# A gather that adds into the node's own rows, and another order of conv 2, in a three-layer graph network kernel

## The chip, the cores and the metric

The kernel runs on one NeuronCore of one Trainium2 chip. The time is device time in microseconds (us) of one launch; smaller is better. Of several runs the median is given.

## What is computed

The graph has 30,000 nodes of 512 float32 features and 30,000 edges, sorted by destination. Three graph convolutions follow each other, each of which multiplies with a 512 x 512 matrix and sums over a node and its incoming edges:

```python
h = jnp.maximum(_layernorm(x, axis=-1), 0.0)
x = x + _L0_gnn_ref(h, ...)      # conv 1 and conv 2, below
h = jnp.maximum(_layernorm(x, axis=-1), 0.0)
x = x + _L1_gnn_ref(h, ...)      # conv 3

# _L0_gnn_ref
h = gcn_conv(x, W1, b1, src, dst, N)
h = layer_norm(h, gamma1, beta1)
h = jax.nn.gelu(h, approximate=False)
h = gcn_conv(h, W2, b2, src, dst, N)
h = layer_norm(h, gamma2, beta2)
return jax.nn.gelu(h + residual, approximate=False)

# gcn_conv
msg = (dinv[s] * dinv[d])[:, None] * (x @ W)[s]
out = jax.ops.segment_sum(msg, d, num_segments=n_nodes) + b
```

`s` and `d` hold the edges and one self-loop for each node.

## The kernel before, in words

Setup (some 440 us) counts degrees, builds lists of the rows to gather, splits the weights into a high and a low float32r part (`Whi`, `Wlo`) and writes the first layer's scaled input `H[0]` to HBM.

Then each convolution goes over 118 pairs of tiles; a pair is 2 x 128 nodes, and p is its number. One step on one pair is called a turn here. The rows are summed before they are multiplied with W:

- SyncE (SP) loads the pair's own rows (`self`, 512 KB), `load_self`; in conv 2 and 3 also rows of x.
- GpSimd (POOL) issues three gathers of 128 rows of 2 KB each, `gather`: for the nodes j = 0 and j = 1 of each partition the row of the node's first edge, and a third one with the rows of all further edges, which reach `v`. It also makes two sums in conv 2 and conv 3 (`residual`) and one small power (`power`) in conv 1 and 2.
- ScalarE (ACT) splits the further edges' rows (`vhi`, `over_high`), splits the aggregate out of PSUM (`ahi`, `high`), and does gelu and relu.
- VectorE (DVE) makes `vlo` and the selection matrix `sv` (`over_low`), the aggregate's low part `alo` (`low`), in conv 1 and conv 3 the add of first edges to own rows (`add_first`), the statistics of a product (`stats`, `mean_var`, `var_eps`), and writes (out - mean) * gamma (`centre`), then `normal`. In conv 2 it makes a second layernorm's sums as well (`x2_sum` to `x2_coefs`). In conv 3 only `result` follows the product.
- TensorE (PE) in `aggregate` transposes the own rows (8 products of 128 columns; 16 in conv 2, where the first edges are transposed and accumulated too) and adds the V products (8 of 256 columns, `sv` with `vhi` and `vlo`). In `multiply` it makes 24 products of 512 columns and, in conv 1 and 2, two more with `root` for the bias.

Each engine has a `body(p, known)` written by hand; what it calls in which order is the engine's program, and one turn calls for pair p + 2 what other functions do for p. TensorE's is:

```python
if has(known, 1):
    aggregate(p.after(1))
if has(known, 0):
    for j in range(2):
        multiply(p, j, known)
```

`stats(p)` waits for `multiply(p)`; the V products of `aggregate(p)` wait for `over_low(p)`; `low(p)` gives `multiply(p)` its last third. Aggregates have two buffers in PSUM, products 2 x 2. At each convolution's start all engines wait for each other.

Of the kernel before, what the change touches and what calls it, by code (L numbers as in the profile page):

```python
# [5 lines left out]
P = 128  # L6
ALU = mybir.AluOpType
# [6 lines left out]
EPS = 1e-5  # L14
# [41 lines left out]
def gnn_kernel(nc, x, src, dst, W1, b1, g1, be1, W2, b2, g2, be2, W3, b3, out):  # L56
# [19 lines left out]
    with ExitStack() as ctx:  # L76
# [48 lines left out]
        ones = sb("ones", [P, P])  # L125
# [8 lines left out]
        neg_half = sb("neg_half", [P, 4])  # L134
        dinv = sb("dinv", [P, NTE])
# [6 lines left out]
        has_first = sb("has_first", [P, NTE])  # L142
# [7 lines left out]
        SelfP = [sb(f"self{u}", [P, 2, D]) for u in range(2)]  # L150
        G = [sb(f"g{u}", [P, 3, D]) for u in range(2)]
# [23 lines left out]
        scr = [g[:, :, :].rearrange("p k d -> p (k d)")[:, k * WINDOW:(k + 1) * WINDOW] for g in G for k in range(4)]  # L175
        edge_place = scr[4][:, 0:3 * NPAIR].rearrange("p (c n) -> p c n", c=3)
        fl = G[1][:, 0, :].rearrange("p (h j) -> p h j", h=2)
        b_hi, b_lo = Vhi[0][0:3, :], G[1][0:3, 1, :]
# [5 lines left out]
        oh_place = [sb(f"oh_place{u}", [P, WINDOW], BF16) for u in range(4)]  # L184
# [10 lines left out]
        stage = [t[:, j, :] for t in SelfP for j in range(2)]  # L195
# [16 lines left out]
        g_clear, zero_out = sem("gathered_cleared"), sem("zeros_out")  # L212
# [28 lines left out]
        with nc.Block() as block:  # L241
            @block.sync
            def _(sp):
# [61 lines left out]
            def _(pool):  # L305
# [22 lines left out]
                pool.wait_ge(win_turned, 1)  # L328
                nc.gpsimd.memset(G[0][:, :, :], 0.0).then_inc(g_clear, 1)
                pool.wait_ge(place_used, 3 * NPAIR)  # L330
                nc.gpsimd.memset(G[1][:, :, :], 0.0)
# [25 lines left out]
            def _(dve):  # L357
# [9 lines left out]
                nc.vector.memset(has_first[:, :], 0.0)  # L367
# [170 lines left out]
                def place(n):  # L538
                    p, c = n // 3, n % 3
                    if n >= 4:  # L540
                        dve.wait_ge(place_used, n - 3)
                    nc.vector.tensor_scalar(oh_place[n % 4][:, :], placeb[:, :], edge_place[:, c, p:p + 1], None,
                                            ALU.is_equal).then_inc(place_made, 1)
# [12 lines left out]
                link(nc.vector.tensor_scalar(row[:, 3:4], row[:, 0:1], float(N), None, ALU.add))  # L556
                for k in range(3):
# [4 lines left out]
                    if k < 2:  # L562
                        nc.vector.tensor_copy(has_first[:, :].rearrange("p (n j) -> p j n", j=2)[:, k, :], tab[:, 3, :])
# [691 lines left out]
```

## Time and profile before

| | us |
|---|---|
| median of 3 runs (3600.72 to 3601.57) | 3601.41 |
| the profiled execution | 3601.81 |
| its span, first to last instruction | 3599.8 |
| TensorE busy | 3057.2 (85%) |
| VectorE busy | 3139.7 (87%) |
| ScalarE busy | 1650.5 (46%) |
| GpSimd busy | 2095.7 (58%) |
| conv 1, about | 440 to 1403 |
| conv 2, about | 1403 to 2558 |
| conv 3, about | 2558 to 3600 |

In the profile's rows PE is TensorE's products, PEld its weight loads, DVE VectorE, ACT ScalarE, POOL GpSimd, SP SyncE. A row of the timeline has the start, the duration, the engine, the line of the kernel, the operation, and what it writes <- reads; `x4` is four instructions of a kind, merged. In brackets stands how long the engine stood idle before, and who released it. Shares are means over stages with different limits, so the stages are read one by one.

### The profile page before, as it was taken

To read this page: it belongs to the slowest core of one execution; us is meant where nothing else is said; L and a number is where in the kernel's file an instruction comes from. 1 tells how busy PE (TensorE), PEld (TensorE's weight loads), DVE (VectorE), ACT (ScalarE), POOL (GpSimd) and SP (SyncE) were. 2 spreads that over 40 slices of the span, in tenths; PEclk is the share of its full clock that TensorE was granted. 3 is DMA by queue.
4 is the path that set the end of the run, shared out by engine and by line. 5 is a ranking of instruction groups with operands and counts; after the bars stand their busy time and mean duration, and the time that the engine had idled before them with its cause. 6 is when DMAs were issued, how large, how long until landed. Compare 5 with 4: busy or idle time off the path is not lost. (4 is left out here: it accounts for less than half of the span.)

```text
span 3599.8 us, 61879 instructions
## 1 busy us (share of the span) xinstructions
PE 3057.2 (85%) x16897; PEld 2498.2 (69%) x16897; DVE 3139.7 (87%) x6745; ACT 1650.5 (46%) x2375; POOL 2095.7 (58%) x1853
## 2 busy tenths in 40 slices
PE   8133299999999997999999999999488888888888
PEld 2022188888888886777777777778477777777777
DVE  9899789999999996888888888888688888888887
ACT  0366445555555553777777777777311111111111
POOL 0122256556556654677777777777466666666665
PEclk9999999999999998999999999999799999999999
DMA  3499967777777775888888888888477777777775
GB/s 118 163 408 418 365 215 221 220 225 222 218 223 223 220 219 171 289 295 299 297 296 295 296 298 295 297 295 288 162 241 246 241 246 242 241 246 238 246 240 190
DMA packets 277302, 914.70 MB, mean 254 GB/s; under 512 B 47617, under 2 KB 49511, under 8 KB 277246
## 3 DMA queue, kind: packets, MB, share of 16 engines
q1 hardware_dynamic: 191614, 683.15, 53.1%
q0 software_dynamic: 85632, 230.90, 22.9%
q8 instruction: 24, 0.39, 0.0%
q14 instruction: 32, 0.26, 0.0%
HBM read 653.47 MB, written 308.59 MB: 267 GB/s over the span
## 5 line engine op out<-in xcount | busy, mean ns | idle before, releaser
L840 POOL DMA_INDIRECT g<-H,idx x1062 | 1212.3, 1142 | 614.8 <-issue 428.9
L895 ACT ACTIVATE ahi<-agg 128x1024 fp32r<-128x1024 f32 x354 | 360.9, 1019 | 1039.1 <-PE agg L1171 1039.1
L1189 PE MATMUL out<-Whi,ahi 128*128 128x512 f32 x2832 | 768.9, 393 | 0.0
L1189 PE MATMUL out<-Wlo,ahi 128*128 128x512 f32 x2832 | 763.6, 391 | 0.0
L1189 PE MATMUL out<-Whi,alo 128*128 128x512 f32 x2832 | 761.2, 391 | 0.5 <-DVE alo L1006 0.5
L1162 PE MATMUL agg<-ident,self 128*128 128x128 f32 x2832 | 474.5, 279 | 220.9 <-DVE self L998 171.9
L1189 PEld LDWEIGHTS out<-Wlo,ahi 128*128 128x128 f32 x2832 | 531.6, 188 | 119.6
L1189 PEld LDWEIGHTS out<-Whi,alo 128*128 128x128 f32 x2832 | 531.6, 188 | 114.1 <-DVE alo L1006 1.0
L1189 PEld LDWEIGHTS out<-Whi,ahi 128*128 128x128 f32 x2832 | 510.4, 189 | 91.1
L1162 PEld LDWEIGHTS agg<-ident,self 128*128 128x128 f32 x2832 | 339.3, 142 | 315.8 <-DVE self L998 220.6
L1171 PE MATMUL agg<-sv,vhi 128*128 128x256 f32 x1416 | 384.0, 304 | 66.2 <-DVE sv L986 66.2
L902 ACT ACTIVATE y<-y 128x1024 f32<-128x1024 f32 x236 | 250.1, 1060 | 403.2 <-DVE y L1052 403.2
L1006 DVE TENSOR_TENSOR alo<-agg,ahi 128x1024 fp32r<-128x1024 f32 x354 | 427.8, 1208 | 7.5 <-ACT ahi L895 7.5
L865 POOL TENSOR_TENSOR small<-small,neg_half 128x2 f32<-128x2 f32 (+1 forms) x237 | 207.9, 877 | 372.5 <-DVE small L1030 366.2
L986 DVE TENSOR_SCALAR sv<-col,over_to 128x256 fp32r<-128x256 f32 x354 | 420.9, 1189 | 0.0
L984 DVE TENSOR_TENSOR vlo<-g,vhi 128x512 fp32r<-128x512 f32 x354 | 248.8, 703 | 183.6 <-ACT vhi L889 183.6
L851 POOL TENSOR_TENSOR r<-r,vec 128x512 f32<-128x512 f32 x236 | 299.7, 1288 | 141.2 <-ACT r L925 141.2
L1171 PE MATMUL agg<-sv,vlo 128*128 128x256 f32 x1416 | 355.3, 283 | 0.0
L1171 PEld LDWEIGHTS agg<-sv,vhi 128*128 128x128 f32 x1416 | 270.5, 191 | 90.0 <-DVE vlo L984 90.0
L1037 DVE SCALAR_TENSOR_TENSOR conv<-out,small,vec 128x512 f32<-128x512 f32 x472 | 331.1, 743 | 0.0
L858 POOL TENSOR_TENSOR r<-x,vec 128x512 f32<-128x512 f32 x236 | 299.1, 1293 | 10.2 <-DVE conv L1097 7.5
L1014 DVE BATCH_NORM_STATS2 small<-out 128x6 f32<-128x512 f32 x472 | 302.6, 679 | 2.0 <-PE out L1194 2.0
(175 smaller groups left out, 4137.5 us busy)
## 6 DMA issues: line engine op xcount, KB each, us to landing
self<-H SPq DMA_DIRECT2D x351, 512.0 KB, 5.1
H<-ho SPq DMA_DIRECT2D x250, 512.0 KB, 4.2
x<-in_x_dram SPq DMA_DIRECT2D x165, 512.0 KB, 6.2
X<-x SPq DMA_DIRECT2D x117, 512.0 KB, 4.3
x<-X SPq DMA_DIRECT2D x117, 512.0 KB, 7.2
out_dram<-conv SPq DMA_DIRECT2D x117, 512.0 KB, 6.3
H<-x SPq DMA_DIRECT2D x48, 512.0 KB, 9.6
g<-H,idx POOLq DMA_INDIRECT x1062, 4.3
```

The costliest lines, as they stand in the source:

```text
L840: pool.indirect_dma_start(g[:, c, :], None, H[q][0:end, :], bass.IndirectOffsetOnAxis(ap=own[:, c:c + 1], axis=0), bounds_check=end - 1, o ...
L851: nc.gpsimd.tensor_tensor(R[:, j, :], R[:, j, :], beta_b[1][:, :], ALU.add)\
L858: nc.gpsimd.tensor_tensor(R[:, j, :], Xt[:, j, :], bias_b[2][:, :], ALU.add)\
L895: nc.scalar.activation(Ahi[p.slot(2)][:, :], Agg[p.slot(2)][:, :], ACT.Copy)\
L902: nc.scalar.activation(y, y, ACT.Gelu).then_inc(gelu_done.sem, 1)
L986: nc.vector.tensor_scalar(Sv[p.slot(2)][:, :], col[:, :], over_to[:, bass.ds(p.n, 1)], None, ALU.is_equal).then_inc(sv_made.sem, 1)
L1006: nc.vector.tensor_tensor(Alo[p.slot(2)][:, :], Agg[p.slot(2)][:, :], Ahi[p.slot(2)][:, :].bitcast(F32), ALU.subtract).then_inc(lo_done.se ...
L1014: s = nc.vector.bn_stats(m[:, 6 * j:6 * j + 6], Out[2 * p.slot(2) + j][:, :])
L1037: nc.vector.scalar_tensor_tensor(CvP[p.slot(2)][:, j, :], Out[2 * p.slot(2) + j][:, :], m[:, 12 + 2 * j:13 + 2 * j], gamma_b[q][:, :], ALU ...
L1162: nc.tensor.matmul(o, own[:, j, fs], ident[:, :], is_transpose=True, start=(f % 2 == 0 and j == 0), stop=False, skip_group_check=True)
L1171: m = nc.tensor.matmul(agg[:, 2 * f * P:2 * (f + 1) * P], V[p.slot(2)][:, f * P:(f + 1) * P], Sv[p.slot(2)][:, :], start=False, stop=(V is ...
L1189: m = nc.tensor.matmul(o, a[u][:, c:c + P], w[q][:, f, :], start=(n == 0), stop=(third and n == 3 * KD - 1))
```

## The change

The gather of first edges becomes an accumulating one: each gathered row is added by the DMA to the node's own row in SBUF, after the own rows have landed (`compute_op` add). Nodes without a first edge get an index out of bounds, which the DMA skips; before, it fetched a row of zeros for them in conv 1 and 2. So `add_first`, the second eight transposes of conv 2 and the writing of zero rows in setup are gone. The own rows get four buffers, not two, and are loaded a turn earlier; the gather waits for `self_in` and `vlo_done`, no longer for the aggregate or the sum. Several `tensor_scalar` of VectorE become `scalar_tensor_tensor` with a tensor of ones, `sv` among them. In conv 1 `low` moves behind `stats`. In conv 2 the bodies of VectorE, ScalarE and GpSimd are written in another order. Setup uses three buffers in place of four for `oh_place`.

```diff
-        SelfP = [sb(f"self{u}", [P, 2, D]) for u in range(2)]
-        G = [sb(f"g{u}", [P, 3, D]) for u in range(2)]
+        gathered = sb("gathered", [P, 10, D])
+        SelfP = [gathered[:, 2 * u:2 * u + 2, :] for u in range(4)]
+        V = [gathered[:, 8 + u, :] for u in range(2)]
...
-                sp.wait_ge(g_clear, 1)
-                for q in range(3):
-                    sp.dma_start(H[q][N:N + P, :], G[0][:, 0, :]).then_inc(zero_out, 16)
-                sp.wait_ge(zero_out, 16 * 3)
...
                     def load_self(known, p, k):
-                        if has(known, k - 2):
-                            sp.wait_ge(agg_done.sem, agg_done.upto(p.after(-2)))
+                        if has(known, k - 4):
...
-                        sp.dma_start(filled(SelfP[p.slot(2)], last), whole(H[q], p.n, last, general_reg * ROWS))\
+                        sp.dma_start(filled(SelfP[p.slot(4)], last), whole(H[q], p.n, last, general_reg * ROWS))\
...
+                        if has(known, 4):
+                            load_self(known, p.after(4), 4)
...
                         if has(known, k - 2):
-                            if added:
-                                pool.wait_ge(sum_done.sem, sum_done.upto(p.after(-2)))
-                                pool.wait_ge(vlo_done.sem, vlo_done.upto(p.after(-2)))
-                            else:
-                                pool.wait_ge(agg_done.sem, agg_done.upto(p.after(-2)))
+                            pool.wait_ge(vlo_done.sem, vlo_done.upto(p.after(-2)))
                         pool.wait_ge(idx_made.sem, idx_made.upto(p))
+                        pool.wait_ge(self_in.of(p), self_in.upto(p))
                         pool.sem_inc(gather_go, 1)
-                        own, g = idx[p.slot(4)], G[p.slot(2)]
-                        for c in range(3):
-                            end = N + P if padded_rows and c < 2 else N
-                            pool.indirect_dma_start(g[:, c, :], None, H[q][0:end, :],
+                        own = idx[p.slot(4)]
+                        rows = [SelfP[p.slot(4)][:, 0, :], SelfP[p.slot(4)][:, 1, :], V[p.slot(2)][:, :]]
+                        for c, op in enumerate((ALU.add, ALU.add, ALU.bypass)):
+                            pool.indirect_dma_start(rows[c], None, H[q][0:N, :],
                                                     bass.IndirectOffsetOnAxis(ap=own[:, c:c + 1], axis=0),
-                                                    bounds_check=end - 1, oob_is_err=False)\
+                                                    bounds_check=N - 1, oob_is_err=False, compute_op=op)\
                                 .then_inc((g_in if c < 2 else v_in).of(p), 16)
 
...
+                            residual(known, p)
+                        if second and (has(known, 0) or has(known, -2)):
+                            power(p)
                         if has(known, 3):
                             gather(known, p.after(3), 3)
-                        if second and has(known, 0):
-                            residual(known, p)
                         if third and has(known, 1):
                             residual(None if known is None else known + 1, p.after(1))
-                        if (first and has(known, 0)) or (second and (has(known, 0) or has(known, -1))):
+                        if first and has(known, 0):
                             power(p)
...
-
-                    def add_first(p):
-
-                        own, g = SelfP[p.slot(2)], G[p.slot(2)]
-                        dve.wait_ge(self_in.of(p), self_in.upto(p))
...
-                                                                   own[:, j, :], ALU.mult, ALU.add)
-                        s.then_inc(sum_done.sem, 1)
+                        nc.vector.scalar_tensor_tensor(Sv[p.slot(2)][:, :], col[:, :], over_to[:, bass.ds(p.n, 1)],
...
                             for k in range(2):
                                 over_low(p.after(k))
-                                if added:
-                                    add_first(p.after(k))
-                            low(p)
-                        if second and has(known, -2):
-                            x2_coefs(p.after(-2))
-                        if not third and has(known, -1):
+                                if k == 0:
+                                    low(p)
+                        if second:
+                            if has(known, 1):
+                                low(p.after(1))
+                            if has(known, 0):
+                                stats(p)
+                                mean_var(p)
+                            if has(known, -2):
+                                v = x2_var_eps(p.after(-2))
+                                if not has(known, 0):
+                                    v.then_inc(ve_done.sem, 1)
+                            if has(known, 0):
+                                var_eps(p)
+                                centre(p)
+                            if has(known, 2):
+                                over_low(p.after(2))
+                            if has(known, -2):
+                                x2_coefs(p.after(-2))
+                            if has(known, 0):
+                                normal(known, p)
+                            if has(known, 4):
+                                indices(p.after(4))
+                            if has(known, -1):
+                                x2_sum(of(known, -1), p.after(-1))
+                                x2_mean(p.after(-1))
...
+                        if first and has(known, -1):
                             normal(of(known, -1), p.after(-1))
                         if has(known, 4):
                             indices(p.after(4))
-                        if has(known, 2):
-                            over_low(p.after(2))
-                            if added:
-                                add_first(p.after(2))
...
                         if has(known, 0):
                             stats(p)
-                        if second and has(known, -1):
...
+                            low(p.after(1))
                         if has(known, 0):
                             mean_var(p)
-                        if second and has(known, -1):
-                            v = x2_var_eps(p.after(-1))
-                            if not has(known, 0):
-                                v.then_inc(ve_done.sem, 1)
```

VectorE, conv 2, before: one turn in the steady part, from the statistics on (`x,small` ahead of it, not shown, is `x2_sum`; `y` is `normal`, `conv` is `centre`):

```order
L1014 BN_STATS small<-out 128x6 x2
L1072 TENSOR_SCALAR small<-small 128x2
L1023 BN_AGGR small<-small 128x2 x2
L1079 TENSOR_SCALAR small<-small 128x2
L1030 TENSOR_TENSOR small<-small,eps 128x2
L1037 SCALAR_TENSOR_TENSOR conv<-out,small,vec 128x512 x2
L1085 TENSOR_TENSOR small<-small,dinv 128x2
L1088 TENSOR_TENSOR small<-small 128x2
L1052 SCALAR_TENSOR_TENSOR y<-conv,small,r 128x512 x2
L978 COPY idx<-rows_from 128x3
L984 TENSOR_TENSOR vlo<-g,vhi 128x512
L986 TENSOR_SCALAR sv<-col,over_to 128x256
```

The same engine and convolution in the changed kernel:

```order
L993 TENSOR_TENSOR alo<-agg,ahi 128x1024
L1001 BN_STATS small<-out 128x6 x2
L1010 BN_AGGR small<-small 128x2 x2
L1066 SCALAR_TENSOR_TENSOR small<-small,eps_c 128x2
L1017 TENSOR_TENSOR small<-small,eps 128x2
L1024 SCALAR_TENSOR_TENSOR conv<-out,small,vec 128x512 x2
L985 TENSOR_TENSOR vlo<-gathered,vhi 128x512
L987 SCALAR_TENSOR_TENSOR sv<-col,over_to,ones 128x256
L1072 TENSOR_TENSOR small<-small,dinv 128x2
L1075 TENSOR_TENSOR small<-small 128x2
L1039 SCALAR_TENSOR_TENSOR y<-conv,small,r 128x512 x2
L979 COPY idx<-rows_from 128x3
```

`alo` of pair p + 1 now opens the turn. `vlo` and `sv` are for pair p + 2 in both, but before they were made in the body ahead of the statistics of p, and now in the same body behind the statistics and `conv` of p.

TensorE, conv 2, in the changed kernel: from the transposes of pair p + 2 to the first product of p + 1, with the semaphores waited for. The order is that of before but for the eight transposes of `g`, which are gone:

```order
L1157 MATMUL agg<-ident,gathered 128x128 [waits g_in3]
L1157 MATMUL agg<-ident,gathered 128x128 x7
L1164 MATMUL agg<-sv,vhi 128x256 [waits sv_made,vlo_done]
L1164 MATMUL agg<-sv,vlo 128x256
L1164 MATMUL agg<-sv,vhi 128x256
L1164 MATMUL agg<-sv,vlo 128x256
L1164 MATMUL agg<-sv,vhi 128x256
L1164 MATMUL agg<-sv,vlo 128x256
L1164 MATMUL agg<-sv,vhi 128x256
L1164 MATMUL agg<-sv,vlo 128x256
L1182 MATMUL out<-Whi,ahi 128x512 [waits cg_done,hi_done]
```

Nothing moved here: TensorE still makes the aggregate of p + 2 between the products of p and those of p + 1.

VectorE, conv 3, before: one turn.

```order
L978 COPY idx<-rows_from 128x3
L984 TENSOR_TENSOR vlo<-g,vhi 128x512
L986 TENSOR_SCALAR sv<-col,over_to 128x256
L998 SCALAR_TENSOR_TENSOR self<-g,has_first,self 128x512 x2
L1006 TENSOR_TENSOR alo<-agg,ahi 128x1024
L1097 SCALAR_TENSOR_TENSOR conv<-out,dinv,r 128x512 x2
```

And in the changed kernel:

```order
L985 TENSOR_TENSOR vlo<-gathered,vhi 128x512
L987 SCALAR_TENSOR_TENSOR sv<-col,over_to,ones 128x256
L979 COPY idx<-rows_from 128x3
L993 TENSOR_TENSOR alo<-agg,ahi 128x1024
L1084 SCALAR_TENSOR_TENSOR conv<-out,dinv,r 128x512 x2
```

The two adds into `self` are gone, `idx` stands behind `sv`, and `sv` reads one tensor more.

## Rows read from the trace of the kernel before

**Rows 1.** Windows of conv 1, 2, 3: busy us (instructions), clock, DMA share, GB/s.

```profile
core 0: us, PE busy (x) PEld busy (x) DVE busy (x) ACT busy (x) POOL busy (x), PEclk, DMA share, GB/s
600.00:900.00 300.00, 299.54 (x1575) 247.59 (x1574) 285.55 (x529) 152.54 (x189) 179.24 (x152) 1.00 0.74 223
1500.00:1800.00 300.00, 281.35 (x1581) 238.59 (x1579) 256.50 (x663) 215.24 (x347) 215.66 (x191) 1.00 0.87 297
2700.00:3000.00 300.00, 260.19 (x1390) 215.12 (x1388) 258.73 (x279) 53.98 (x70) 191.24 (x173) 1.00 0.75 243
```

**Rows 2.** Timeline of conv 1, TensorE: transposes of two turns early and two late.

```profile
502.39 1.03 PE L1162 MATMUL agg<-ident,self 128*128 128x128 f32 x8
...
510.21 1.03 PE L1162 MATMUL agg<-ident,self 128*128 128x128 f32 x8
...
1300.02 1.09 PE L1162 MATMUL agg<-ident,self 128*128 128x128 f32 x8
...
1307.97 1.09 PE L1162 MATMUL agg<-ident,self 128*128 128x128 f32 x8
```

**Rows 3.** Timeline of one turn of conv 2, TensorE and VectorE.

```profile
1903.15 0.68 DVE L984 TENSOR_TENSOR vlo<-g,vhi 128x512 fp32r<-128x512 f32 x1
...
1903.75 0.38 DVE L986 TENSOR_SCALAR sv<-col,over_to 128x256 fp32r<-128x256 f32 x1
...
1904.27 0.36 PE L1171 MATMUL agg<-sv,vhi 128*128 128x256 f32 x1 [0.57 <-DVE sv L986]
...
1906.39 1.28 DVE L1014 BATCH_NORM_STATS2 small<-out 128x6 f32<-128x512 f32 x2
...
1911.05 0.40 PE L1194 MATMUL out<-B,root 128*128 128x512 f32 x1
...
1911.29 0.27 PE L1162 MATMUL agg<-ident,self 128*128 128x128 f32 x1
...
1913.77 0.35 PE L1171 MATMUL agg<-sv,vhi 128*128 128x256 f32 x1 [0.57 <-DVE sv L986]
```

**Rows 4.** Timeline of conv 1's end: TensorE's last product, VectorE behind it.

```profile
1392.98 0.39 PE L1194 MATMUL out<-B,root 128*128 128x512 f32 x1
...
1393.41 0.70 DVE L1014 BATCH_NORM_STATS2 small<-out 128x6 f32<-128x512 f32 x1 [1.28 <-PE out L1194]
...
1394.61 1.40 DVE L1037 SCALAR_TENSOR_TENSOR conv<-out,small,vec 128x512 f32<-128x512 f32 x2
```

**Rows 5.** Timeline of one turn of conv 3.

```profile
2957.59 2.96 DVE L986 TENSOR_SCALAR sv<-col,over_to 128x256 fp32r<-128x256 f32 x1
2957.84 2.55 POOL L858 TENSOR_TENSOR r<-x,vec 128x512 f32<-128x512 f32 x2
...
2961.93 1.09 PE L1162 MATMUL agg<-ident,self 128*128 128x128 f32 x8 [1.09 <-DVE self L998]
```

**Rows 6.** Windows of one microsecond around changes of the granted clock.

```profile
1395.00:1396.00 1.00, 0.00 (x0) 0.00 (x0) 1.00 (x2) 0.00 (x0) 0.47 (x1) 0.71 1.00 414
1419.00:1420.00 1.00, 1.00 (x10) 1.00 (x9) 0.00 (x0) 0.89 (x1) 0.03 (x1) 0.84 0.00 0
2586.00:2587.00 1.00, 0.00 (x0) 0.00 (x0) 1.00 (x1) 0.00 (x0) 1.00 (x2) 0.84 0.65 248
2593.00:2594.00 1.00, 1.00 (x5) 0.80 (x5) 0.00 (x0) 0.82 (x1) 0.97 (x2) 0.75 0.49 131
```

**Rows 7.** Timeline: TensorE's first products after two long idle stretches.

```profile
1413.72 0.45 PE L1162 MATMUL agg<-ident,self 128*128 128x128 f32 x1 [20.35 <-DMA g<-H,idx]
...
2589.47 1.97 PE L1162 MATMUL agg<-ident,self 128*128 128x128 f32 x8 [5.29 <-DVE self L998]
```

**Rows 8.** Groups of GpSimd, conv 3, 2900 to 3100: busy, mean ns | idle before.

```profile
L840 POOL DMA_INDIRECT g<-H,idx x69 | 69.2, 1002 | 70.9 <-issue 41.7 <-DVE self L998 29.2
```

**Rows 9.** DMA queues of the same stretch: packets, MB, share of 16 engines.

```profile
q1 hardware_dynamic: 10063, 36.66, 54.5%
q0 software_dynamic: 5517, 12.15, 20.6%
```

**Rows 10.** DMA issues of the page: size, us from issue to landing.

```profile
self<-H SPq DMA_DIRECT2D x351, 512.0 KB, 5.1
```

More of the change, by code:

```diff
@@ L734, in convolution @@
             first, second, third = q == 0, q == 1, q == 2
-            added = not second
-            padded_rows = not third
             lag = 2 if second else 1
@@ L810, in body @@
                             load_x(known, p.after(2), 2)
-                        if has(known, 3):
-                            load_self(known, p.after(3), 3)
                         if has(known, -lag):
@@ L847, in residual @@
                         R, Xt = RP[p.slot(2)], XtP[p.slot(4)]
+                        if second and has(known, -2):
+                            pool.wait_ge(mean2_done.sem, mean2_done.upto(p.after(-2)))
                         for j in range(2):
@@ L928, in squares @@
                     def squares(p):
-                        m = small[p.after(1).slot(4)]
+                        m = small[p.after(2).slot(4)]
                         for j in range(2):
@@ L938, in relu_x2 @@
                     def relu_x2(known, p):
-                        m = small[p.after(1).slot(4)]
+                        m = small[p.after(2).slot(4)]
                         wait_stored(known, p)
@@ L1056, in x2_sum @@
                     def x2_sum(known, p):
-                        m = small[p.after(1).slot(4)]
+                        m = small[p.after(2).slot(4)]
                         dve.wait_ge(gelu_done.sem, gelu_done.upto(p))
@@ L1132, in body @@
                             stats(p)
-                        if second and has(known, -1):
-                            x2_mean(p.after(-1))
+                        if has(known, 1):
+                            low(p.after(1))
                         if has(known, 0):
                             mean_var(p)
-                        if second and has(known, -1):
-                            v = x2_var_eps(p.after(-1))
-                            if not has(known, 0):
-                                v.then_inc(ve_done.sem, 1)
-                        if has(known, 0):
                             var_eps(p)
@@ L1210, in convolution @@
                 landed.close()
-            if added:
-                sum_done.close()
             if not third:
@@ L1216, in convolution @@
                 for flag in (ve_done, rstd_done):
-                    flag.close(NPAIR + second)
+                    flag.close(NPAIR + 2 * second)
                 root_in.close()
```

146 lines of the change are left out of this document (70 added, 76 removed).

## The prediction

> **What bounds the kernel now.** I read the windows first. In conv 1 TensorE is busy 299.5 of 300 us, in conv 2 281.4, in conv 3 260.2, while VectorE has 285.6, 256.5 and 258.7 [rows 1]. A "turn" below is the work on one pair of tiles; each convolution has 118. TensorE issues 42, 50 and 40 products a turn, so the counts of the windows give turns of 8.00, 9.49 and 8.63 us.
>
> Then the timeline, for what each turn waits on. Conv 1 is TensorE itself: where nothing holds it a turn is 510.21 - 502.39 = 7.82 us, later 1307.97 - 1300.02 = 7.95 because the own rows wait a little for VectorE's add [rows 2]. In conv 2 a turn is 1913.77 - 1904.27 = 9.50 us. The wait that ends last is TensorE's for `sv` (0.57 us at line 1171) [rows 3]. The reader should note one thing more there: VectorE starts its statistics at 1906.39, and they read the product whose last instruction (`root`) stood a turn before 1911.05, at 1901.55. VectorE comes more than four microseconds behind TensorE, so TensorE does not wait for statistics. In conv 3, `sv` takes 2.96 us while GpSimd makes its two sums (2.55 us), the adds of first edges come behind it, and TensorE's transposes wait 1.09 us for them [rows 5].
>
> **The change, part by part.**
>
> *Conv 1.* The add goes, with nothing in its place on a compute engine. TensorE's floor of 7.82 us stays. From about 7.97 (between 7.95 and 8.00) that is 0.15 us a turn. I count 115 full turns a convolution, the other three being fill and drain: -17 us. `low` now comes behind the statistics: 0.70 us for these, and at most 1.4 for an operation of twice centre's 0.70 [rows 4], while TensorE has its transposes (7.82 - 6.78 - 0.24 = 0.80 us), the V products and eight products of 0.24 us before it needs `alo`, over 3 us; nothing is lost.
>
> *Conv 2, the order.* Eight transposes a turn go (16 x 0.11 us becomes 8 x 0.11), which frees TensorE by 0.86 us. But `over_low(p+2)`, which stood ahead of `stats(p)` on VectorE, now stands behind `centre(p)`. On TensorE, unchanged, `aggregate(p+2)` stands ahead of `multiply(p+1)` and its V products wait for `vlo` and `sv` of p+2. So: multiply(p) ends, stats(p), means, centre(p), over_low(p+2), V products of p+2, multiply(p+1), stats(p+1). That is a circle of one turn, and nothing in it overlaps. Its length, from starts of instructions:
> - last product's start (`root`) to stats: 1393.41 - 1392.98 = 0.43; stats to the end of centre: 1394.61 + 1.40 - 1393.41 = 2.60. These come from the end of conv 1, where VectorE really waits for TensorE [rows 4];
> - one more tiny operation, `x2_var_eps`: 0.10, my estimate;
> - `vlo` to the start of `sv`: 1903.75 - 1903.15 = 0.60 [rows 3]; `sv` now reads two tensors: between its 0.38 and the 0.70 of a centre operation of twice the size [rows 3, 4], I take 0.45; less 0.07 since an operation starts before the last ends;
> - end of `sv` to the first V product: 1904.27 - 1904.13 = 0.14; V products and the multiply to the last `root`: 1911.05 - 1904.27 = 6.78 [rows 3].
>
> The sum is 0.43 + 2.60 + 0.10 + 0.60 + 0.45 - 0.07 + 0.14 + 6.78 = 11.03, with small waits 11.05 us. Against 9.50 that is 1.55 x 115 = +178 us. VectorE's own 8.1 us a turn (256.5/300 x 9.49) and GpSimd's work fit inside, and gathers issued behind `power(p)` have two turns to land. The bounds are 10.9 and 11.3 us.
>
> *Conv 2, the clock.* In this circle TensorE stands idle for 0.43 + 2.60 + 0.10 + 0.98 + 0.14 = 4.25 us from the last root's start, less the 0.24 us to the next instruction and the 1.09 us of eight transposes [rows 5]: 2.9 us in one piece, every turn. In the profile the granted clock fell to half 2.05 us after TensorE's last product (ended 1393.37; the mean 0.71 of 1395 to 1396 puts the fall at 1395.42), and elsewhere 2.5 us after (2589.47 - 5.29 = 2584.18; fall at 2586.68) [rows 4, 6, 7]. After a restart it stayed at half for 4.0 us (2589.47 to 2593.5) and 5.6 us (1413.72 to 1419.3) [rows 6, 7]. At half, eight transposes take 1.97 us, not 1.09 [rows 5, 7]. Waits of 1.1 us in conv 3 never brought it down (1.00) [rows 1, 5]. 2.9 us are longer than both stretches that did, so I expect falls in most turns. Half of 4.0 to 5.6 us is 2.0 to 2.8 us lost by each; some turns will be spared, so I take 1.6 us a turn: +184 us. Bounds: 0, and 2.6 us a turn (+299).
>
> *Conv 3.* The adds go, and `sv` no longer holds up anything TensorE needs: VectorE's 258.7/300 x 8.63 = 7.4 us a turn [rows 1] lose the adds, 1.4 us from the end of `sv` (2960.55) to 2961.93 [rows 5], so even with `sv` at 2.96 us it has 6.0. TensorE's floor is conv 1's less two roots: 7.82 - 2 x 0.24 = 7.34 us [rows 2, 3]. Now DMA. In the stretch read, the queues take 54.5 + 20.6 = 75.1% of 8.63 = 6.5 us, of which gathers are 1.8 us [rows 9]. How long an accumulating gather takes no row shows; a plain one is the nearest. If it is the same, 6.5; if all gathers double, 8.3 us. GpSimd has 3 x 1.00 for gathers, 2.55 for sums and up to 1.8 us (41.7/23) of issue gaps [rows 5, 8], 7.35 us at most if an accumulating issue costs 1.00; if two of three double, 9.3. I take 7.45 us: 1.18 x 115 = -136 us. The bounds are -148 (7.34) and 0.
>
> The Trainium skill, page "Collectives: The Full Stack", section "The bandwidth ceiling: the fold count and why AG ≠ RS ≠ AR", says that an adding transfer needs two source reads and so gets half the rate of a copy. No row here shows an accumulating transfer. By that rule conv 3 would be limited by DMA near the 8.3 us above rather than by TensorE; it is the third rival.
>
> *Starts and setup.* At each of three starts the first gather now waits for its own rows, which take 5.1 us to land [rows 10]; between 0 and 5.1, I take 3.5 each, less the first add (1.4, by conv 3's) in two of them, less about 2 us for the zero rows no longer written after setup: +6 us.
>
> **Sum:** -17 + 178 + 184 - 136 + 6 = +215. Against the profiled execution's own 3601.8 us (span 3599.8, with 2 us around it; the median is 3601.4, the same) this is 3817 us.
>
> **Rivals.**
> - *The clock holds* in conv 2. For it: the granted clock is 1.00 through all full turns now. Against it: the falls after 2.05 and 2.5 us. It gives 3817 - 184 = 3633 us. Chance 0.12.
> - *The clock stays at half through most of each turn*, as the 5.6 us after a restart allow: 6.78 us of work becomes up to 13.6. At 5 us a turn lost: 3817 + 391 = 4208 us. Chance 0.05.
> - *The accumulating gathers cost conv 3 its gain* (doubled transfer or issue; decided at 8.3 us or more a turn): 3817 + (8.3 - 7.45) x 115 = 3915 us, and 3953 with no gain at all. Chance 0.12.
> - *Faster:* the circle does not close, because VectorE's `over_low` is done before TensorE comes to the V products, and conv 2 runs at VectorE's 8.1 us or so. For it: 0.86 us of TensorE's work is gone and VectorE has the time. Against it: the order rows leave no way past `stats`. With the clock held, 3633 - (11.05 - 8.2) x 115 = 3305 us. It decides from a turn of 10.8 us down: without the clock's price all else sums to -147, so conv 2 may lose 1.28 us a turn. Chance 0.05.
>
> The forecast has 0.66.
>
> **How the numbers follow.** The forecast's own spread is 3700 to 3940: clock 1.1 to 2.6 us a turn (-58, +115), circle 10.9 to 11.3 (-17, +29). With most of the third rival this holds about 0.75 to 0.8; the held clock below and the rest above are left out. A measurement here can tell 0.2% (7 us). Faster by more: the last rival and a little of the first, 0.06; within: 0.02; slower: 0.92.
>
> **What the changed profile would show.** In conv 2, VectorE's statistics begin 0.04 us after TensorE's `root` ends, and TensorE's V products wait about 3 us for `sv`, in every turn; a turn is above 11 us. The granted clock of conv 2 is below 1.00 (some 0.75 to 0.9). Conv 1's turn is 7.8, conv 3's 7.4 to 7.5, with no wait for own rows; the accumulating issues last about 1.0 us. I am wrong if statistics find their product long finished, if the granted clock is 1.00 in conv 2 (then by 184), or if conv 3's transposes wait for a gather.

## The result, and the profile after

The changed kernel takes 3898.99 us (median of 4 runs, 3884.15 to 3913.64) against 3601.49 for the kernel before (4 runs): 1.083 times as long, 95% interval 1.079 to 1.087. The forecast had the direction and its reasons in conv 2, and was 82 us too low. The windows of the changed kernel, columns as in [rows 1]:

```profile
900.00:1200.00 300.00, 297.79 (x1597) 252.43 (x1596) 243.34 (x491) 148.19 (x190) 193.47 (x152) 1.00 0.77 199
1500.00:1800.00 300.00, 227.02 (x1034) 187.31 (x1033) 206.33 (x511) 168.41 (x272) 207.78 (x148) 0.89 0.73 215
1800.00:2100.00 300.00, 227.05 (x994) 187.56 (x993) 203.04 (x503) 162.91 (x261) 201.78 (x144) 0.85 0.71 208
3100.00:3400.00 300.00, 274.64 (x1453) 232.41 (x1453) 186.45 (x219) 59.81 (x74) 241.98 (x181) 0.98 0.85 253
```

TensorE now issues 42, 42 and 40 products a turn, so conv 1 takes 300 / (1597/42) = 7.89 us a turn, conv 3 8.26, and conv 2, with the groups of 1500 to 2800 us below (314 gathers, three a turn, in 1300 us), 12.4. With 115 full turns each, against 7.97, 8.63 and 9.50 before: -9, -43 and +335, together +283 of the 297 us measured. TensorE's granted clock is 0.85 to 0.89 in conv 2 (a mean over its two levels) and a little below 1.00 in conv 3.

One turn of conv 2, TensorE and VectorE (the idle time before an instruction and who ended it in brackets):

```profile
2001.12 0.40 PE L1187 MATMUL out<-B,root 128*128 128x512 f32 x1
...
2001.56 0.70 DVE L1001 BATCH_NORM_STATS2 small<-out 128x6 f32<-128x512 f32 x1 [2.29 <-PE out L1187]
...
2002.86 1.40 DVE L1024 SCALAR_TENSOR_TENSOR conv<-out,small,vec 128x512 f32<-128x512 f32 x2
...
2004.78 0.48 DVE L987 SCALAR_TENSOR_TENSOR sv<-col,over_to,ones 128x256 fp32r<-128x256 f32 x1
...
2005.40 0.36 PE L1164 MATMUL agg<-sv,vhi 128*128 128x256 f32 x1 [3.01 <-DVE sv L987]
...
2012.16 0.40 PE L1187 MATMUL out<-B,root 128*128 128x512 f32 x1
```

This is the circle, with the order of the forecast: root, statistics, centre, `sv`, V products, the next root 11.04 us later. In [rows 3] VectorE's statistics came more than 4 us behind TensorE; here VectorE waits for TensorE, then TensorE 3.01 us for VectorE. The turn shown ran at full clock; the mean is 1.4 us longer.

Two turns of conv 3, where the forecast's largest miss is (compare [rows 5]):

```profile
3302.99 1.03 POOL L827 DMA_INDIRECT gathered<-H,idx  x1 [0.31 <-issue]
...
3310.74 0.63 ACT L880 ACTIVATE vhi<-gathered 128x512 fp32r<-128x512 f32 x1 [2.78 <-DMA gathered<-H,idx]
...
3311.40 3.18 DVE L985 TENSOR_TENSOR vlo<-gathered,vhi 128x512 fp32r<-128x512 f32 x1 [5.35 <-ACT vhi L880]
3311.51 2.51 POOL L847 TENSOR_TENSOR r<-x,vec 128x512 f32<-128x512 f32 x2
...
3315.12 0.35 PE L1164 MATMUL agg<-sv,vhi 128*128 128x256 f32 x1 [1.89 <-DVE sv L987]
...
3315.99 1.55 POOL L827 DMA_INDIRECT gathered<-H,idx  x1 [1.97 <-DVE idx L979]
```

The further edges' rows are issued third, at 3302.99, behind two adding gathers; `vhi` can begin 7.75 us later; `vlo` then lasts 3.18 us instead of 0.69, since GpSimd makes its sums (2.51) at that moment; only behind `vlo` and `sv` come the indices and the next gathers. TensorE does not wait for `sv` in every turn, but from 3000 to 3800 us 39 times in 97 turns. In groups, 1500 to 2800 us (conv 2) and 3000 to 3800 us (conv 3):

```profile
L827 POOL DMA_INDIRECT gathered<-H,idx x314 | 509.6, 1623 | 84.2 <-issue 52.1 <-DVE small L1059 32.0
L1164 PE MATMUL agg<-sv,vhi 128*128 128x256 f32 x416 | 136.4, 350 | 316.1 <-DVE sv L987 316.1
```

```profile
L827 POOL DMA_INDIRECT gathered<-H,idx x291 | 404.6, 1390 | 152.4 <-DVE idx L979 86.6 <-issue 62.8 <-DVE vlo L985 3.0
L1164 PE MATMUL agg<-sv,vhi 128*128 128x256 f32 x388 | 108.2, 310 | 65.5 <-DVE sv L987 65.4
L985 DVE TENSOR_TENSOR vlo<-gathered,vhi 128x512 fp32r<-128x512 f32 x97 | 156.8, 1616 | 261.1 <-ACT vhi L880 247.2 <-issue 13.9
```

A gather is issued in 1.39 us on the mean of conv 3 (adding ones 1.55, plain 1.03) and 1.62 in conv 2, against 1.00 in [rows 8].

### The profile page after: what moved, and what is told of

The parts are those of the page before. It is cut to its first block and busy times, and to the rows that moved or that the text cites. A ratio compares the mean times of both kernels' runs of the same rounds, so it can differ in the third digit from the quotient of the medians.

```text
span 3897.6 us, 59104 instructions
## 1 busy us (share of the span) xinstructions
PE 3110.9 (80%) x15953; PEld 2552.1 (65%) x15953; DVE 2764.7 (71%) x6388; ACT 1643.4 (42%) x2375; POOL 2461.3 (63%) x1854
## 5 line engine op out<-in xcount | busy, mean ns | idle before, releaser
L827 POOL DMA_INDIRECT gathered<-H,idx x1062 | 1579.0, 1487 | 429.0 <-issue 249.3
L1182 PE MATMUL out<-Whi,ahi 128*128 128x512 f32 x2832 | 830.5, 418 | 0.0
L1182 PE MATMUL out<-Wlo,ahi 128*128 128x512 f32 x2832 | 826.7, 417 | 0.0
L1164 PE MATMUL agg<-sv,vhi 128*128 128x256 f32 x1416 | 415.0, 322 | 438.4 <-DVE sv L987 438.3
L985 DVE TENSOR_TENSOR vlo<-gathered,vhi 128x512 fp32r<-128x512 f32 x354 | 351.9, 994 | 496.1 <-ACT vhi L880 480.6
L1182 PEld LDWEIGHTS out<-Wlo,ahi 128*128 128x128 f32 x2832 | 579.4, 205 | 135.1
L1182 PEld LDWEIGHTS out<-Whi,ahi 128*128 128x128 f32 x2832 | 543.7, 202 | 98.8
L880 ACT ACTIVATE vhi<-gathered 128x512 fp32r<-128x512 f32 x354 | 222.6, 629 | 561.9 <-DMA gathered<-H,idx 554.2
L1157 PE MATMUL agg<-ident,gathered 128*128 128x128 f32 x2832 | 372.7, 275 | 86.0 <-DMA gathered<-H,idx 86.0
L1157 PEld LDWEIGHTS agg<-ident,gathered 128*128 128x128 f32 x2832 | 336.4, 142 | 133.6 <-DMA gathered<-H,idx 87.4
```

The costliest lines, as they stand in the source:

```text
L827: pool.indirect_dma_start(rows[c], None, H[q][0:N, :], bass.IndirectOffsetOnAxis(ap=own[:, c:c + 1], axis=0), bounds_check=N - 1, oob_is_e ...
L880: nc.scalar.activation(Vhi[p.slot(2)][:, :], V[p.slot(2)][:, :], ACT.Copy)\
L985: nc.vector.tensor_tensor(Vlo[p.slot(2)][:, :], V[p.slot(2)][:, :], Vhi[p.slot(2)][:, :].bitcast(F32), ALU.subtract).then_inc(vlo_done.sem, 1)
L1157: nc.tensor.matmul(agg[:, (2 * f + j) * P:(2 * f + j + 1) * P], own[:, j, fs], ident[:, :], is_transpose=True, start=(f % 2 == 0 and j == ...
L1164: m = nc.tensor.matmul(agg[:, 2 * f * P:2 * (f + 1) * P], part[p.slot(2)][:, f * P:(f + 1) * P], Sv[p.slot(2)][:, :], start=False, stop=(p ...
L1182: m = nc.tensor.matmul(o, a[u][:, c:c + P], w[q][:, f, :], start=(n == 0), stop=(third and n == 3 * KD - 1))
```

## The experiments

My theory after the result: conv 2 is held by the circle (11.04 us) and on top of it by a fallen clock (1.4 us); conv 3 by the chain over two turns shown above. The rivals: the clock has no part in it, or the accumulating transfers slow every stage by themselves.

**The clock alone.** Conv 2's transposes are made three times over the same PSUM, which fills 2.06 us of TensorE's wait and leaves the circle alone:

```diff
-                        for f in range(KD):
+                        for _ in range(3 if second else 1):
+                            for f in range(KD):
```

> The changed kernel, with conv 2's eight transposes of own rows made three times over the same PSUM (the result is the same), so that TensorE works 2.06 us of the 3.0 us in which it waits for sv; the circle is as before. Theory (the circle of 11.04 us and, apart from it, a fallen clock): the granted clock of conv 2 is 1.00, its turn 11.04 to 11.1 instead of 12.4 us, 3899 - 1.35 x 115 = 3744 us (3725 to 3770). Rival (the extra time over 11.04 us is not the clock but late rows or transfers): no change or up to 60 us slower.

Measured: 3737.60 us (4 runs), 1.037 of before (1.036 to 1.039), 161 us less than the changed kernel. Its window:

```profile
1800.00:2100.00 300.00, 264.52 (x1575) 228.70 (x1572) 229.17 (x570) 186.09 (x300) 229.76 (x164) 1.00 0.80 239
```

With 58 products a turn that is 11.05 us, at a clock of 1.00. So the clock cost 1.4 us a turn, 161 us, and the circle is 11.05 us without it. More work on TensorE made the kernel faster.

**VectorE's order alone, then GpSimd's too.** `over_low(p + 2)` moves ahead of `stats(p)`:

```diff
+                            if has(known, 2):
+                                over_low(p.after(2))
                             if has(known, 0):
                                 stats(p)
...
                                 centre(p)
-                            if has(known, 2):
-                                over_low(p.after(2))
```

> The changed kernel with one move: conv 2's over_low(p + 2) stands ahead of stats(p) on VectorE. My theory: this opens the circle of 11.04 us through TensorE (V products no longer wait for stats), but GpSimd still gathers behind power(p - 1), so another circle closes: var_eps(p - 1) at 2002.78, third gather issued at 2008.69, its rows in vhi at 2014.02, then vlo and sv 1.1 us, statistics to var_eps 1.9 us: 14.3 us a turn less what the sum hides, so 13.9 to 14.5 us a turn in conv 2 and about 4080 us (4030 to 4130) in all; VectorE then waits for vhi ahead of vlo in every turn. Rival (the place on VectorE is all that matters): VectorE's own 8.7 us a turn, TensorE's clock back at 1.00, about 3470 us.

In the second kernel GpSimd's `gather(p + 3)` also moves ahead of `residual(p)` and `power(p)`.

> As the run before, and GpSimd's gather(p + 3) of conv 2 also stands ahead of the sums and the power of turn p. My theory: both circles are open; the longest engine is then GpSimd with gathers 2.08 + 1.75 + 1.05, gaps 0.8, sums 2.55, power 1.04 and its wait 0.2: 9.5 us a turn (9.3 to 10.0), against 12.4 in the changed kernel, clock 0.97 or more: 3899 - 2.9 x 115 = 3565 us (3540 to 3640). Rival (the circle is not the cause, conv 2 is held by its transfers or by the sum of its waits): within 1% of 3899 us. The rival that GpSimd does not bind either gives VectorE's 8.7 us and 3475 us.

Measured: 4346.73 us (one run) and 3802.60 us (1.056 of before, 1.054 to 1.058). The windows of conv 2, in this order:

```profile
1800.00:2100.00 300.00, 201.97 (x767) 163.09 (x766) 153.72 (x388) 128.89 (x201) 148.99 (x110) 0.73 0.52 158
```

```profile
1800.00:2100.00 300.00, 229.74 (x1083) 190.78 (x1082) 269.31 (x542) 179.64 (x285) 202.59 (x154) 0.91 0.75 225
```

16.4 and 11.6 us a turn, where I expected about 14.2 and 9.5. In the first the circle that I named did close, and was longer: the last gather issued at 2020.80, `vhi` at 2028.37, 7.6 us instead of the 4.7 I had read in one turn. For the second, GpSimd and VectorE tell why:

```profile
2007.34 2.52 POOL L840 TENSOR_TENSOR r<-r,vec 128x512 f32<-128x512 f32 x2
2007.54 2.35 DVE L1066 SCALAR_TENSOR_TENSOR small<-small,eps_c 128x2 f32<-128x2 f32 x1
2009.81 0.15 DVE L1017 TENSOR_TENSOR small<-small,eps 128x2 f32<-128x2 f32 x1
2010.04 1.04 POOL L854 TENSOR_TENSOR small<-small,neg_half 128x4 f32<-128x4 f32 x1 [0.18 <-DVE small L1017]
```

`x2_var_eps`, two numbers a partition, stands 2.35 us until GpSimd's sums end. `power`, `centre`, `normal`, the indices and the next gathers come behind it. The circle through TensorE is open, and one through GpSimd's sums has closed. The 2.2 us by which `x2_var_eps` is longer than its 0.15 are about as much as the turn is above the 9.5 I expected. The operation has its new form here (`scalar_tensor_tensor`); what that does to it comes up below, with the gather without the order.

**The adding alone.** All gathers are plain (the own rows are overwritten, the adding is left out):

```diff
-                        for c, op in enumerate((ALU.add, ALU.add, ALU.bypass)):
+                        for c, op in enumerate((ALU.bypass, ALU.bypass, ALU.bypass)):
```

> The changed kernel with first edges gathered by a plain copy: their rows replace the node's own rows, and the adding is left out; the same rows move from DRAM. It prices the adding. Theory (the longer issue on GpSimd is what the adding costs): issues fall from 1.5 to 2.0 us to 1.0; conv 3's chain over two turns (issues, landing 6.7 us, vhi, vlo, sv, next gather) loses 1.0 us and more if rows land sooner, so conv 3 falls from 8.25 to 7.5 to 7.8 us a turn (-50 to -85 us); conv 1 from 7.89 to 7.82 (-8); conv 2 does not change, since its circle holds no gather: 3806 to 3841 us. Rival (the adding transfer is bound by DRAM or queue bandwidth): landing falls much too, conv 2 too, below 3780. Rival (adding costs nothing, the sums' place costs): within 10 us of 3899.

Measured: 3798.69 us (3788.46 to 3825.70), 7 us below the range I gave; the profiled execution is the one of 3825.70. Conv 3's window, and its gathers and queue of 3100 to 3500 us:

```profile
3100.00:3400.00 300.00, 288.15 (x1544) 243.09 (x1543) 242.19 (x232) 63.08 (x76) 215.18 (x193) 1.00 0.82 271
```

```profile
L827 POOL DMA_INDIRECT gathered<-H,idx x155 | 158.0, 1020 | 110.7 <-DVE idx L979 76.2 <-issue 34.5
```

```profile
q0 software_dynamic: 12335, 27.19, 23.8%
```

Conv 3 takes 7.77 us a turn: the adding costs 0.5 us there, 56 us of the forecast's 93 us miss. Conv 2 does not gain (12.5 us from 1500 to 2700 us against 12.4). The gathers' queue takes 23.8% of 7.77 = 1.85 us a turn; the same stretch of the changed kernel has

```profile
q0 software_dynamic: 17668, 25.39, 32.4%
```

32.4% of 8.26 = 2.68 us. If the plain third gather takes 0.62 us in both, an adding one takes 1.7 times a plain one. That speaks for the direction of the rule of half the rate that the prediction quotes from the Trainium skill, page "Collectives: The Full Stack", section "The bandwidth ceiling: the fold count and why AG ≠ RS ≠ AR". But TensorE, not DMA, is at 288 of 300 us here, and in the changed kernel DMA is at 0.85: the adding reached the time through GpSimd's issue and the place of its sums, not by a full DMA.

**Conv 3's chain.** The rows of further edges are gathered first; in a second kernel the sums also wait for `sv`, and VectorE copies the indices at the head of its turn:

```diff
-                        for c, op in enumerate((ALU.add, ALU.add, ALU.bypass)):
+                        for c, op in ((2, ALU.bypass), (0, ALU.add), (1, ALU.add)):
...
+                        if third and has(known, 2):
+                            pool.wait_ge(sv_made.sem, sv_made.upto(p.after(2)))
                         if third and has(known, 1):
                             residual(None if known is None else known + 1, p.after(1))
```

> The changed kernel, with GpSimd issuing the plain gather of overflow rows first and the two adding ones after it. Theory: conv 3 is held by a chain over two turns: vlo(p + 1), three issues, 6.7 us to landing, vhi(p + 3), vlo(p + 3), 16.5 us; the rows are issued 3.7 us sooner, the chain is 12.8 us, and conv 3 falls from 8.25 us a turn to GpSimd's and TensorE's 7.45, or to 7.9 as long as GpSimd's sums still hold vlo: -40 to -92 us; conv 2 the same: 3807 to 3860 us, 3830 the likeliest. Rival (GpSimd's own length or the DRAM side holds conv 3): within 10 us of 3899.

> As the run before, and in conv 3 VectorE copies the indices at the head of its turn, and GpSimd's sums wait for sv, so that they run beside VectorE's low and result, which read PSUM. Theory: an operation of VectorE that reads only SBUF stands still while GpSimd's sums run (vlo 3.2 to 3.8 us instead of 0.69, sv 3.2 instead of 0.48); now none does (vlo mean 0.69, sv 0.48), conv 3 runs at 7.5 us a turn (7.4 to 7.6): 3899 - 0.75 x 115 = 3813 us, and if the run before stays at 7.9, this one is 45 us faster than it. Rival (the standstill is hidden once rows come early): no more than 8 us between the two.

Measured: 3770.17 us (1.046, 1.044 to 1.048), 37 us below the range I gave, and 3763.75 us (1.045, 1.043 to 1.047), 49 us below what I expected. Conv 3's windows:

```profile
3100.00:3400.00 300.00, 289.19 (x1556) 244.65 (x1555) 165.51 (x234) 60.58 (x78) 270.04 (x196) 0.99 0.95 273
```

```profile
3100.00:3400.00 300.00, 286.31 (x1542) 242.48 (x1541) 217.80 (x232) 58.99 (x76) 270.19 (x195) 0.99 0.94 272
```

7.71 and 7.78 us a turn. The chain was right: the same three gathers in another order give back 0.55 us of each turn, and TensorE waits no longer for `sv`. The second kernel gained no turn time, and its rival holds. But its edit did not end the standstill, it moved it: from 3000 to 3600 us `vlo` takes 0.95 us on the mean instead of 1.27, and the copy of the indices, now at the head of the turn, 1.66 instead of 0.16. VectorE stands 1.2 us a turn longer than in the first kernel and the turn is no longer, so once rows come early a standstill of this size is off the path. What a turn without any is worth, no run shows. Of the first one's 129 us, conv 3 explains 63 and conv 1 (7.78 us a turn) 13. The rest is conv 2, which fell by 0.5 us a turn though its circle holds no gather: its clock is higher (0.90 to 0.93 in three windows). There TensorE's idle stretch is in two pieces: from 1500 to 2700 us its transposes wait 0.7 us a turn for the adding gathers, which now come last, and its V products 2.2 us for `sv` instead of 3.0. That this is why the clock falls less I did not test.

**The gather without the order.** Conv 2's bodies are in the order of the kernel before, all else is as in the changed one, also the new form (`scalar_tensor_tensor`) of `sv`, `x2_mean` and `x2_var_eps`; then one wait more:

```diff
                         R, Xt = RP[p.slot(2)], XtP[p.slot(4)]
+                        if second and has(known, -1):
+                            pool.wait_ge(mean2_done.sem, mean2_done.upto(p.after(-1)))
```

> The other half of the change alone: first edges gathered into the own rows in all three convolutions (with the larger rings and the new form of sv), conv 2's order on VectorE, ScalarE and GpSimd as in the kernel before. My theory: the order alone made conv 2 slow; without it conv 1 gains 9 us and conv 3 40 us as in the changed kernel, and conv 2 loses its eight transposes of first rows on TensorE (0.9 us), of which half shows, 9.0 us a turn (8.7 to 9.5) at a clock of 1.00: 3601 - 9 - 57 - 40 = 3495 us (3440 to 3555). Rival (the accumulating gather slows conv 2 as well, by its longer issues on GpSimd): conv 2 at 10 us a turn or more, 3610 us or more.

> The gather alone, and conv 2's sums on GpSimd wait for x2_mean(p - 1). Theory: in the gather alone x2_mean stands 1.76 us still behind the sums, since the longer issues bring them late; ScalarE's squares, x2_var_eps, power and the next gathers wait behind it, a circle of 11.25 us. With the wait x2_mean is out of the way, the squares run beside the sums, and x2_var_eps stands still until the sums end instead: power to power 10.7 us (10.4 to 10.9), -0.55 x 115 = -63 us and some for the clock: 3680 us (3640 to 3705). Rival (it is the transfers or the issues themselves that make conv 2 long): within 10 us of 3754, or slower, since GpSimd starts its sums 0.9 us later.

Measured: 3754.57 us (1.042, 1.040 to 1.043), 260 us above what I expected, and 3671.72 us (1.020, 1.018 to 1.021), as expected. In the first (conv 2, 11.2 us a turn):

```profile
2004.67 2.55 POOL L838 TENSOR_TENSOR r<-r,vec 128x512 f32<-128x512 f32 x2
...
2005.48 1.77 DVE L1046 SCALAR_TENSOR_TENSOR small<-small,ones 128x2 f32<-128x2 f32 x1
...
2007.28 0.72 ACT L921 ACTIVATE y<-x,small 128x512 f32<-128x512 f32 x1 [2.43 <-DVE small L1046]
...
2009.18 1.04 POOL L852 TENSOR_TENSOR small<-small,neg_half 128x4 f32<-128x4 f32 x1 [1.96 <-DVE small L1004]
```

`x2_mean` starts 0.8 us after the sums and stands until they end; ScalarE's squares wait 2.43 us for it, and `power` and the next gathers come behind them. I had laid this to the longer issues (4.8 us for three, 3.3 before), which bring the sums late, on top of `x2_mean`. The rows of the kernel before speak against it:

```profile
1906.46 2.54 POOL L851 TENSOR_TENSOR r<-r,vec 128x512 f32<-128x512 f32 x2 [1.12 <-ACT r L925]
...
1907.60 0.17 DVE L1072 TENSOR_SCALAR small<-small 128x2 f32<-128x2 f32 x1
```

```profile
L1072 DVE TENSOR_SCALAR small<-small x105: 147/163/178, 1508.3 to 2496.9; 128x2 f32<-128x2 f32 x105
```

and of the gather without the order, the same operation:

```profile
L1046 DVE SCALAR_TENSOR_TENSOR small<-small,ones x90: 1734/1760/1776, 1501.4 to 2498.4; 128x2 f32<-128x2 f32 x90
```

The sums lay on top of `x2_mean` before, too: in 116 of the 118 turns it starts inside them, and it takes 0.16 us all the same. What differs is its form, `tensor_scalar` before and `scalar_tensor_tensor` with a tensor of ones now. And it is on a circle: in the kernel before `power` follows `power` after 9.5 us in every turn (1900.21 to 1909.71), through VectorE's operations from `x2_coefs` to `x2_mean`, the squares and `x2_var_eps`, each of which begins within 0.2 us of the end of the one before. The 1.6 us that `x2_mean` stands make it 11.2.

With the added wait `x2_mean` is free again (0.15 us), but the sums now catch `x2_var_eps`, which takes 1.15 us instead of 0.16; 9.5 and 1.0 us are the 10.5 us a turn of this kernel, 0.7 less than without the wait. So the rows put most of what conv 2 loses in these two kernels on the new form of two small operations, and little on the gather: with the sums at their old place the new form would stand until 1909.00, 1.4 us (an estimate from the rows above), which leaves 0.4 us for the later sums. This is read from the rows and not shown by a run: the accumulating gather with the old form in conv 2 was not tried.

**All moves together.** The kernel with conv 3's two edits, and in conv 2 `indices`, `over_low(p + 2)` and `low(p + 1)` ahead of `stats(p)`, `over_high` ahead of the squares, the gather first, and sums that wait for `sv`.

> All together, to beat both kernels: as the run before, and in conv 2 VectorE's turn begins with the indices, over_low(p + 2) and low(p + 1) ahead of stats(p), ScalarE's over_high(p + 2) stands ahead of the squares, GpSimd gathers first, and its sums wait for sv(p + 2), beside low and stats. Theory: no circle through TensorE is left, x2_var_eps no longer stands behind the sums (2.36 us where only the gather and over_low were moved), and GpSimd's own length of 9.3 us sets conv 2: 9.5 to 9.8 us a turn, clock 0.97 or more: 3601 - 12 + 17 - 130 = 3476 us (3440 to 3535). Rival (GpSimd's wait for sv closes another circle): conv 2 at 10.5 or more, 3590 us or more.

Measured: 3553.83 us (0.987 of before, 0.985 to 0.988): faster than both kernels, 78 us above what I expected. Conv 2 takes 10.15 us a turn. The circle through TensorE is open, but GpSimd's first gather waits for the own rows it adds to. Of the waits of 1600 to 2400 us (us in total, times, longest):

```profile
POOL gathered L827 <- DMA gathered<-H: 83.2, 45, 3.3
```

That is about 1 us a turn, a wait that a plain gather does not have. The second cause in sight is `x2_var_eps` in its new form, 1.57 us on the mean of the same stretch:

```profile
L1068 DVE SCALAR_TENSOR_TENSOR small<-small,eps_c 128x2 f32<-128x2 f32 x79 | 123.8, 1567 | 0.0
```

No run separates the two.

**The adding only where it pays.** From the kernel before: the accumulating gather in conv 1 and conv 3 (further edges first), conv 2 untouched.

```diff
+            ring = 4 if added else 2
...
+                        if added:
+                            own, mine = idx[p.slot(4)], Own[p.slot(4)]
+                            for c in (2, 0, 1):
+                                pool.indirect_dma_start(Over[p.slot(2)][:, :] if c == 2 else mine[:, c, :], None,
...
+                                                        compute_op=ALU.bypass if c == 2 else ALU.add)\
```

> The kernel before, with the accumulating gather in conv 1 and conv 3 alone (own rows four pairs deep, overflow rows gathered first, no add on VectorE); conv 2 keeps its plain gathers, its second set of transposes and its order. Theory: the accumulating gather pays where VectorE's add was on the path and costs where it pushes GpSimd's sums later; conv 1 at 7.82 us a turn (-17), conv 2 at 9.50 as before, conv 3 at 7.75 instead of 8.63 (-101): 3603 - 118 + 6 = 3490 us (3465 to 3520). Rival (the gain of conv 3 needs the new form of sv, whose old form stands 2.94 us behind the sums here): conv 3 at 8.1 or more, 3530 us or more.

Measured: 3474.39 us (5 runs, 3471.56 to 3476.93), 0.965 of before (0.963 to 0.966), the fastest kernel of this study.

```profile
900.00:1200.00 300.00, 300.00 (x1610) 255.98 (x1609) 252.29 (x500) 152.35 (x193) 202.44 (x154) 1.00 0.77 201
...
1800.00:2100.00 300.00, 281.25 (x1583) 238.80 (x1582) 256.98 (x665) 215.25 (x347) 215.46 (x190) 1.00 0.86 296
...
3000.00:3300.00 300.00, 287.77 (x1554) 243.95 (x1553) 198.12 (x234) 59.88 (x77) 270.03 (x196) 0.99 0.93 271
```

The old forms stay in this kernel: `x2_mean` takes 0.16 us in conv 2, and with `sv` as `tensor_scalar` conv 3 is as short as with the new form, so its gain does not need it. Conv 1 takes 7.83 us a turn, conv 2 9.48 as before, conv 3 7.72: (7.83 - 7.97) x 115 - (8.63 - 7.72) x 115 = -121 of the 127 us measured.

## Why the prediction was right in direction and 82 us low

The measured time lies in the stated spread, 3700 to 3940 us. That is in part luck: conv 3 alone missed by 93 us, and conv 2 with its clock was 27 us shorter than forecast, which hid a part of it.

- **Conv 2, the order** (+178 forecast): right. The circle is 11.04 us in the trace and 11.05 where the clock holds, against 11.05: +178. Its signs came too: statistics 0.04 us after `root` ends, a wait of 3.01 us for `sv`.
- **Conv 2, the clock** (+184): right in mechanism, 1.4 us a turn instead of 1.6. The experiment with added transposes measures it: 161 us.
- **Conv 3** (-136): the term that failed. It measured -43. The bounds 0 and -148 held it, but I took a value near TensorE's floor since "an accumulating issue costs 1.00"; it costs 1.55 there (up to 2.08 in conv 2). I had also reckoned each engine's length and not the chain over two turns: three issues, landing, `vhi`, `vlo`, `sv`, indices. Plain gathers give 0.5 us of the missing 0.8; gathering the further edges first gives 0.55 with the adding kept. I had named "conv 3's transposes wait for a gather" as the sign; it was the V products, which wait for `sv` behind a gather. The sentence that `sv` "no longer holds up anything TensorE needs" was wrong.
- **Conv 1** (-17): -9; `low` is sometimes late behind `over_low`, whose rows land late, and TensorE then waits for `alo` (5.0 us in 101 turns); the other 0.02 us has no row. With the further edges gathered first it takes 7.8 us.
- **Starts** (+6): what is left of the sum, 297 - 283 = +14; not measured by itself.
- **The rivals.** The rival that adding costs conv 3 its gain (3915 us) came nearest: it has conv 3 at 8.3 us, and 8.26 was measured. I gave its price to a doubled transfer or issue and 0.12; the issues are 1.5 to 2 times as long. Its 8.3 us for DMA doubled all three gathers, though one of them is plain: two doubled give 6.5 + 2/3 x 1.8 = 7.7 us, and the queues were busy for 0.85 x 8.26 = 7.0 us, so DMA did not limit the turn. With conv 3 at 8.26 and all else as forecast the sum is 3910 us. The held clock, the clock at half most of the turn, and the open circle did not occur.
- **What no step had.** The prediction read TensorE's wait of 0.57 us for `sv` as what holds conv 2 before. The rows show the circle of 9.5 us through `power`, VectorE and the squares. Nor did it ask what the new form does to a small operation beside GpSimd's sums; that plays no part in the changed kernel's conv 2, but it does in the experiments'. With the order of before, new form and gather together cost conv 2 1.7 us a turn, and the rows put most of it on `x2_mean` standing still; the new order keeps `x2_mean` and `x2_var_eps` clear of the sums (0.16 and 0.14 us), at the price of a circle through TensorE. Whether the adding gather with the old forms gains in conv 2 stays open: the best of the kernels with the new form is 0.65 us a turn above the plain gathers.

## What to carry to other kernels

Before moving an operation behind another engine's result, write down the circle of one turn: who waits for it, and whether that engine's next turn must pass it; 0.5 us of wait became 3 us here. An operation that saves an engine work but lengthens another engine's queue is priced by what then falls on top of what, not by its own length; try it stage by stage, and keep it where the saved work was on the path. When two kernels differ in several ways, look up the form of each small operation too: one of two numbers a partition, written another way, took 1.76 us instead of 0.16. Where TensorE idles in every turn, the granted clock is a second cost on top of the wait.

## What the runs showed of the hardware

- While GpSimd makes its sums, some operations of VectorE that read only SBUF stand still until the sums end, however small: a copy of 3 numbers a partition took up to 3.2 us instead of 0.16, `sv` 3.21 as `scalar_tensor_tensor` instead of 0.48 and 2.96 as `tensor_scalar` instead of 0.38, `vlo` 3.7 instead of 0.69, a `scalar_tensor_tensor` of 2 numbers 1.76 (`x2_mean`) and 2.35 (`x2_var_eps`) instead of 0.16. Not held, though they read only SBUF, were `x2_mean` as `tensor_scalar` (0.16 us, 116 of 118 turns of the kernel before) and `bn_aggr` of 6 numbers (at most 0.18 us, same kernel). Those with an input from PSUM are not held either. The changed kernel's rows of 3000 to 3600 us (ns, shortest/median/longest):

```profile
L987 DVE SCALAR_TENSOR_TENSOR sv<-col,over_to,ones x72: 471/479/3214, 3003.7 to 3596.2; 128x256 fp32r<-128x256 f32 x72
```

```profile
L993 DVE TENSOR_TENSOR alo<-agg,ahi x73: 1208/1211/1219, 2999.5 to 3596.6; 128x1024 fp32r<-128x1024 f32 x73
L1084 DVE SCALAR_TENSOR_TENSOR conv<-out,dinv,r x146: 734/739/752, 3000.7 to 3598.4; 128x512 f32<-128x512 f32 x146
```

Of the last two 7 and 45 lie beside the sums.

The Trainium skill, "GPSIMD Engine Reference", section "1. Specifications", names contention with VectorE's instructions in a 2-port mode or with two SBUF inputs. The traces agree for `vlo` and for `sv`, `x2_mean` and `x2_var_eps` as `scalar_tensor_tensor`, which have two such inputs and were held, and for `alo` and `x2_mean` as `tensor_scalar`, which have one and were not; the mode of the copy, and of `sv` as `tensor_scalar`, no row shows.

- An accumulating indirect DMA of 128 rows of 2 KB took 1.55 us to issue in conv 3 of the changed kernel and up to 2.08 in conv 2, the plain one behind them 1.03 and 1.05 (1.00 in [rows 8]; 1.28 on the mean where it is issued first). It took about 1.7 times the queue's time, an estimate worked out above.
- 2.06 us of repeated work on TensorE in a wait of 3.0 us raised the mean granted clock of conv 2 from 0.85 to 0.89 up to 1.00 and made the kernel 161 us faster.
